# Attention: two units' weighted sums in one bank, one copy and one turn; the packs a place sooner, the causal masks in front of the wait for them

## The reference

```python
def _L0_attn_ref(x, W_Q, W_K, W_V, W_O):
    H, d_attn = 16, 8
    Q, K, V = x @ W_Q.T, x @ W_K.T, x @ W_V.T      # each then cut into 16 heads of 8
    attn = jnp.einsum('bhqd,bhkd->bhqk', Q, K) * scale
    attn = jnp.where(causal, attn, -jnp.inf)
    probs = jax.nn.softmax(attn, axis=-1)
    y = jnp.einsum('bhqk,bhkd->bhqd', probs, V)
    y = y.transpose(0, 2, 1, 3).reshape(Bx, Sx, Dm)
    return y @ W_O.T
```

## Time and profile before

| | |
|---|---|
| three runs | 1208.91, 1215.56, 1223.81 us; median 1215.56 |
| the profiled execution | 1208.36 us, of which its span is 1205.8 us |
| PE busy | 1106.7 us, 92% of the span |
| DVE busy | 1001.9 us, 83% |
| ACT busy | 789.6 us, 65% |
| POOL busy | 562.8 us, 47% |
| first mixture, attention, second mixture | about 330, 563 and 313 us (from 0, 330 and 893 us) |

### The profile page before, as it was taken

How to read it: one execution, slowest core, us unless ns; L and a number is a source line. 1 busy time by engine, 2 the same in 40 slices (tenths; PEclk the granted TensorE clock), 3 DMA queues, 4 the chain that set the end, 5 groups by cost and what they waited for, 6 DMA issues and landing times. The chain is left out here.

```text
span 1205.8 us, 31981 instructions
## 1 busy us (share of the span) xinstructions
PE 1106.7 (92%) x11588; PEld 683.5 (57%) x11588; DVE 1001.9 (83%) x2589; ACT 789.6 (65%) x1545; POOL 562.8 (47%) x722
## 2 busy tenths in 40 slices
PE   2899999999979989989999989989979999999998
PEld 1566666666525555555555555555545666666665
DVE  5889899898767888888888888888858898898985
ACT  4676767767526676676766766676646767666664
POOL 2566666666503233333333323333325666666655
PEclk9899999999968999999999999999988999999999
DMA  4442443432200000000000000000004434435333
GB/s 127 152 158 86 155 135 105 141 110 104 71 1 1 2 2 2 1 2 2 2 2 2 2 2 2 1 2 2 2 2 142 154 109 136 132 110 158 117 123 97
DMA packets 59865, 80.11 MB, mean 66 GB/s; under 512 B 5568, under 2 KB 26944, under 8 KB 59712
## 3 DMA queue, kind: packets, MB, share of 16 engines
q1 hardware_dynamic: 59712, 78.08, 20.5%
HBM read 73.34 MB, written 4.72 MB: 65 GB/s over the span
## 5 line engine op out<-in xcount | busy, mean ns | idle before, releaser
L696 POOL TENSOR_TENSOR h_lo<-h,h_hi 128x512 f16<-128x512 f32 x288 | 333.2, 1157 | 234.6 <-ACT h_hi L643 232.5
L1256 POOL TENSOR_SCALAR_AFFINE_SELECT probs_at<-probs_at 128x512 f32<-128x512 f32 x256 | 156.3, 634 | 343.9 <-ACT probs_at L1214 343.9
L1136 DVE TENSOR_REDUCE neg_max_at<-score_at 128x2 f16<-128x512 f32 (+1 forms) x384 | 253.9, 690 | 69.9 <-PE score_at L966 64.6
L1214 ACT ACTIVATE probs_at<-prob_at 128x512 f32<-128x512 f32 x384 | 201.7, 599 | 78.3 <-PE prob_at L998 76.4
L635 ACT ACTIVATE a<-a 128x512 f32<-128x512 f32 x256 | 149.0, 582 | 130.5 <-PE a L547 125.6
L435 DVE TENSOR_TENSOR prod<-a,gate_wide 128x512 f32<-128x512 f32 x256 | 175.9, 687 | 48.2 <-ACT a L635 46.6
L563 PE MATMUL y_b<-w_hi,h_hi 128*128 128x128 f16 x1152 | 208.2, 219 | 2.6 <-POOL h_lo L696 2.6
L563 PE MATMUL y_b<-w_lo,h_hi 128*128 128x128 f16 x1152 | 208.1, 219 | 0.0
L563 PE MATMUL y_b<-w_hi,h_lo 128*128 128x128 f16 x1152 | 208.0, 219 | 0.0
L643 ACT ACTIVATE h_hi<-h 128x512 f16<-128x512 f32 x288 | 179.5, 623 | 17.4 <-DVE h L445 16.7
L445 DVE TENSOR_TENSOR h<-prod,b 128x512 f32<-128x512 f32 x256 | 174.4, 681 | 5.3 <-issue 0.4
(11 more groups left out here) (139 smaller groups left out, 1960.0 us busy)
## 6 DMA issues: line engine op xcount, KB each, us to landing
gate_wide<-gate_rows SPq DMA_DIRECT2D x256, 256.0 KB, 5.4
x<-in_L_attn_x_dram SPq DMA_DIRECT2D x16, 256.0 KB, 6.1
out_dram<-x SPq DMA_DIRECT2D x16, 256.0 KB, 6.9
raw_w<-in_L_ffn_w_dram SPq DMA_DIRECT2D x3, 512.0 KB, 4.9
gate_rows<-gate_rows SPq DMA_DIRECT2D x32, 16.0 KB, 1.4
raw_w<-in_L_ffn_sw_dram SPq DMA_DIRECT2D x3, 64.0 KB, 3.6
raw_attn<-in_L_attn_W_Q_dram SPq DMA_DIRECT2D x1, 64.0 KB, 4.7
raw_attn<-in_L_attn_W_K_dram SPq DMA_DIRECT2D x1, 64.0 KB, 3.5
```

The source lines that it names most:

```text
L696: nc.gpsimd.tensor_tensor(h_lo[k][:, :], h[k][:, :], h_hi[k][:, :], ALU.subtract).then_inc(hlo_done, 1)
L1136: nc.vector.tensor_reduce(dst, src, AX.X, ALU.max, negate=True).then_inc(max_done, 1)
L1214: nc.scalar.activation(probs[j % 2][:, i, :], prob_bank[i][:, :], ACT.Exp, scale=SCALE).then_inc(exp_done, 1)
L1256: nc.gpsimd.affine_select(out=p, in_=p, compare_op=ALU.is_ge, fill=0.0, base=0, pattern=[[0, GROUPS], [1, P]], channel_multiplier=-1).then ...
```

## The change

Units j = 0, 1 and units j = 2, 3 of a sequence now share one filling of `o_bank`. `v_ones` keeps its size, but a head of an even unit has its 8 values and its one in the first 16 of its 32 columns and zeros in the other 16, a head of an odd unit the other way round (`v_places`). The odd unit's `weigh` adds to what the even one left; ACT copies after the odd unit only, `o_t` has half the size, and an `o` job has two transposes instead of four. The transposed heads then stand in another order: the division writes `y` in the order of the pairs, and W_O is loaded with its columns in that order, in two transfers with runs of 16 floats. In `PLACES` `o11` goes to the end of unit 2, and `Q00`, `K00`, `Q01`, `K01` move up by a place or more. The wait for the packs moves behind the masks (`packs_ready`).

```diff
+OUT_ROWS = ROWS // 2
...
-            sp.dma_start(self.raw["attn"][:, i, :], self.attn[n]).then_inc(self.loaded["attn"], DMA)
+            src, dst = self.attn[n], self.raw["attn"][:, i, :]
+            if n != "wo":
+                sp.dma_start(dst, src).then_inc(self.loaded["attn"], DMA)
+                continue
+
+            src = src.rearrange("p (g j d) -> p j g d", g=GROUPS, j=UNITS // 2)
+            dst = dst.rearrange("p (j g d) -> p j g d", g=GROUPS, j=UNITS // 2)
+            for j in range(UNITS // 2):
+                sp.dma_start(dst[:, j, :, :], src[:, j, :, :]).then_inc(self.loaded["attn"], DMA)
...
-PLACES = (((), ("q",), ("k",)), (("o10",), ("o11",), ("Q00",)), (("K00",), ("Q01",), ("K01",)),
+PLACES = (((), ("q",), ("k",)), (("o10",), ("Q00",), ("K00",)), (("Q01", "K01"), (), ("o11",)),
           (("m10", "m11"), ("y1",), ()),
           (("z1",), ("Q10",), ("K10",)), (("o00",), ("o01",), ("Q11",)), (("K11",), ("y0",), ("v",)),
           (("m00", "m01"), ("x",), ("z0",)))
...
+        def v_places(slot):
+
+            return v_ones[slot][:, :, :, :].rearrange("p t (n i) (k r) -> p (t n) (i k) r", i=2, r=OUT_ROWS)
...
-                    pe.wait_ge(o_done, c * 2 * UNITS + (b + 1) * UNITS)
+                    pe.wait_ge(o_done, (2 * c + b + 1) * UNITS // 2)
                     dst, done = begin(c, name)
-                    for j in range(UNITS):
+                    for i in range(UNITS // 2):
...
             def begin_scores(c, b, j, i):
 
-                if j == 0 and i == 0:
-
-                    wait_taken(pe, c, f"Q{b}1")
-                    wait_taken(pe, c, f"K{b}1")
...
+            def packs_ready(c, b, j):
+                if j == 0:
+                    wait_taken(pe, c, f"Q{b}1")
+                    wait_taken(pe, c, f"K{b}1")
...
                 parts = [begin_scores(later, later_b, later_j, i) for i in range(2)]
+                packs_ready(later, later_b, later_j)
...
                 pe.wait_ge(masked, unit * 2 + 2)
-                wait_count(pe, o_done, unit)
+                if j % 2 == 0:
+                    wait_count(pe, o_done, unit // 2)
...
-                                                start=(t == 0), stop=(t == 1), skip_group_check=True)
+                                                start=(t == 0 and j % 2 == 0), stop=(t == 1 and j % 2 == 1),
+                                                skip_group_check=True)
...
+                    o = src[:, 0:HEADS * OUT_ROWS].rearrange("p (h r) -> p h r", r=OUT_ROWS)
+                    nc.vector.reciprocal(inv[:, t, :], o[:, :, HEAD]).then_inc(inv_done, 1)
...
-                nc.vector.memset(v[:, :, HEAD + 1:ROWS], 0.0)
-                last = nc.vector.memset(v[:, :, HEAD:HEAD + 1], 1.0)
+                v = v_places(s)
+                nc.vector.memset(v[:, :, 1:3, :].rearrange("p n i r -> p n (i r)"), 0.0)
+                nc.vector.memset(v[:, :, 0:4:3, HEAD + 1:OUT_ROWS], 0.0)
+                last = nc.vector.memset(v[:, :, 0:4:3, HEAD:HEAD + 1], 1.0)
...
                 unit = c * 2 * UNITS + b * UNITS + j
+                if j % 2 == 0:
+                    return
                 act.wait_ge(pv_done, unit + 1)
```

More of the change, by code:

```diff
@@ L159, in load @@
         for i, n in enumerate(self.attn):
-            sp.dma_start(self.raw["attn"][:, i, :], self.attn[n]).then_inc(self.loaded["attn"], DMA)
+            src, dst = self.attn[n], self.raw["attn"][:, i, :]
[6 more added lines that the diff above has]
+                sp.dma_start(dst[:, j, :, :], src[:, j, :, :]).then_inc(self.loaded["attn"], DMA)
     def loads(self, name):
-        return {"router": 1, "attn": len(self.attn)}.get(name, 2) * DMA
+        return {"router": 1, "attn": len(self.attn) - 1 + UNITS // 2}.get(name, 2) * DMA
     def pool_consts(self, pool):
@@ L806, in attention_phase @@
         probs = [sb(f"probs{s}", [P, 3, CHUNK], F32) for s in range(2)]
-        o_t = [sb(f"o_t{s}", [P, UNITS, SEQ], F32) for s in range(2)]
-        inv = sb("inv", [P, 2, UNITS, GROUPS], F32)
+        o_t = [sb(f"o_t{s}", [P, UNITS // 2, SEQ], F32) for s in range(2)]
+        inv = sb("inv", [P, 2, HEADS], F32)
         y = sb("y", [P, 2, P], F32)
@@ L909, in job @@
                     b, t = int(name[1]), int(name[2])
-                    pe.wait_ge(o_done, c * 2 * UNITS + (b + 1) * UNITS)
+                    pe.wait_ge(o_done, (2 * c + b + 1) * UNITS // 2)
                     dst, done = begin(c, name)
-                    for j in range(UNITS):
-                        last = nc.tensor.transpose(dst[:, j * P:(j + 1) * P], o_t[b][:, j, t * P:(t + 1) * P],
+                    for i in range(UNITS // 2):
+                        last = nc.tensor.transpose(dst[:, i * P:(i + 1) * P], o_t[b][:, i, t * P:(t + 1) * P],
                                                    ident[:, :])
@@ L975, in scores @@
                     part = begin_scores(c, b, j, i)
+                    if i == 0:
+                        packs_ready(c, b, j)
                     for h in range(len(part[1])):
@@ L1111, in job @@
                     b, t = int(name[1]), int(name[2])
-                    o = src[:, :].rearrange("p (j g r) -> p j g r", j=UNITS, r=ROWS)
-                    nc.vector.reciprocal(inv[:, t, :, :], o[:, :, :, HEAD]).then_inc(inv_done, 1)
+                    o = src[:, 0:HEADS * OUT_ROWS].rearrange("p (h r) -> p h r", r=OUT_ROWS)
+                    nc.vector.reciprocal(inv[:, t, :], o[:, :, HEAD]).then_inc(inv_done, 1)
                     dve.wait_ge(inv_done, c * 4 + 2 * b + t + 1)
[L1115 to L1118, removed]
+                    last = nc.vector.tensor_tensor(y[:, t, :].rearrange("p (h d) -> p h d", d=HEAD), o[:, :, 0:HEAD],
+                                                   inv[:, t, :].unsqueeze(2).to_broadcast([P, HEADS, HEAD]), ALU.mult)
                 elif kind == "y":
@@ L1157, in _ @@
                 nc.vector.memset(neg_max[s][:, :, :, :, :].rearrange("p a b c d -> p (a b c d)"), 0.0)
-                v = v_ones[s][:, :, :, :].rearrange("p t h r -> p (t h) r")
-                nc.vector.memset(v[:, :, HEAD + 1:ROWS], 0.0)
-                last = nc.vector.memset(v[:, :, HEAD:HEAD + 1], 1.0)
+                v = v_places(s)
+                nc.vector.memset(v[:, :, 1:3, :].rearrange("p n i r -> p n (i r)"), 0.0)
+                nc.vector.memset(v[:, :, 0:4:3, HEAD + 1:OUT_ROWS], 0.0)
+                last = nc.vector.memset(v[:, :, 0:4:3, HEAD:HEAD + 1], 1.0)
             last.then_inc(buffers_set, 1)
@@ L1199, in job @@
                 elif kind == "v":
-                    nc.scalar.activation(v_ones[slot][:, :, :, 0:HEAD],
-                                         src[:, :].rearrange("p (t h d) -> p t h d", t=TILES, d=HEAD),
+                    nc.scalar.activation(v_places(slot)[:, :, 0:4:3, 0:HEAD],
+                                         src[:, :].rearrange("p (n i d) -> p n i d", i=2, d=HEAD),
                                          ACT.Copy).then_inc(done, 1)
@@ L1218, in take_o @@
                 unit = c * 2 * UNITS + b * UNITS + j
+                if j % 2 == 0:
+                    return
                 act.wait_ge(pv_done, unit + 1)
-                nc.scalar.activation(o_t[b][:, j, :], o_bank[:, 0:SEQ], ACT.Copy).then_inc(o_done, 1)
+                nc.scalar.activation(o_t[b][:, j // 2, :], o_bank[:, 0:SEQ], ACT.Copy).then_inc(o_done, 1)
             def turn(c, slot):
```

## The result

The changed kernel takes **1242.43 us** (median of 6 runs, 1229.1 to 1244.0); the kernel before, run beside it, 1213.91 us. The ratio, taken over the runs and not from the two medians, is 1.0191, with a 95% interval of 1.0155 to 1.0227: slower, though not certainly by 2%, where 1196 us and a range of 1181 to 1210 were forecast. The profiled execution took 1242.43 us, 34.1 us more than the one before.

The account below looks back on a forecast made before the run. PE (91% busy) looked like the bound, with DVE (83%) close behind. From 1208.4 us, -16.5 - 0.5 + 0.8 + 0.4 gave 1192.6; half of a 7.2 us median offset on top made 1196 us, range 1181 to 1210.

Parts of the forecast that it names:

- Units 1 and 2, the fewer transposes: Fewer transposes in `o10` and `o11` gain nothing, because PE then waits for DVE's maximum.
- the sum: Whole kernel: -16.5 - 0.5 + 0.8 + 0.4 = -15.8 us, so 1192.6 us for an execution like the profiled one.
- W_O's short runs: Rival: W_O's load delays x of the second chunk by some 27 us; 1219 us, up to 1226; chance 4%.
- The packs: Unit 2 to unit 3: packs ready sooner, 0.8 us a turn; 0.2 us of the wait turn into one for DVE.
- Unit 5: Two transposes fewer in `o00`, where PE sets the pace: 0.29 us a turn; nothing from `o01`.
- The last turn: No packs made there; fewer transposes and copies in front of unit 6's exponents: 0.5 us, between 0 and 1.
- W_O, +0.8 us: W_O's load in 64-byte runs delays the second chunk's x: 0.8 us added, between 0 and 1.8.
- the estimate of +0.3: W_O's load by the skill's packet overhead: 2.1 times its time before, some +0.3 us, the sum 0.5 us lower.
- The zeros of `v_ones`: Two instructions instead of one per buffer, in front of ACT's first job: 0.4 us added, between 0 and 0.8.
- What would show it: Signs: masks' `q_pack_at` wait from 14.2 to under 2 us, `neg_max_at` from 16.2 to 25; 128 transposes, 64 copies.
- The forecast's own range: Whole kernel, 1187 to 1203 us: 0.7 to 1.25 us a chunk, added parts at either end, offset 0 to 7.2.

Follow-up runs that it names:

- run 10: Changed kernel plus nine matmuls that nobody reads, in TensorE's wait in front of `o10`: 1194.38 us, ratio 0.9865 to the kernel before.
- run 2: Kernel before with only the new order (`PLACES`) and the masks in front of the pack wait: 1201.65 us, ratio 0.9889.
- run 3: Changed kernel in which each `o` job turns its two tiles twice, 128 useless transposes more: 1199.03 us, ratio 0.9870.
- run 5: Changed kernel with the second pair of transposes put back as waste in `o10` and `o11` alone: 1198.33 us, ratio 0.9867.
- run 1: Changed kernel with the old order and the masks behind the pack wait, so only the shared sums are left: 1242.45 us, ratio 1.0248.
- run 4: Kernel before with only two of four transposes in `o10` and `o11`, DVE reading the two tiles twice: 1250.86 us, ratio 1.0304.
- run 9: Kernel before plus six filling matmuls in front of `o10`, as a control: 1218.96 us, ratio 1.0035.
- run 11: Changed kernel plus six filling matmuls in front of `o10` and 24 of 512 columns before the attention's first `Q00`: 1197.93 us, ratio 0.9892.

## Why the prediction was wrong, by its steps

**The step that failed** is "Units 1 and 2, the fewer transposes": "I cost these edits at nothing; what is late next is the maximum." By waits this was right. From the turn's `xt_hi` copy to unit 2's heads it was 9.97 us before (604.90 less 594.93) and is 9.98 in run 10 (599.11 less 589.13). But the step took the granted clock of 1.00 in the earlier trace rows for a given, and the work that it removed was what held it. With the clock held, 15 turns take 487.8 us (run 10, 359.7 to 847.5); the changed kernel took 537.4. These 49.6 us are the term that the sum lacked. No rival named the clock, and the one that ended slower, W_O's short runs, had the wrong mechanism.

**The rest of the sum holds at full clock.** Run 10's 15 turns are 16.2 us shorter than before's 504.0, where 16.5 was forecast, and its profiled execution of 1192.2 us stands beside the sum of 1192.6. Its nine matmuls are its only difference from the changed kernel, and they are hidden. That the totals agree to 0.4 us is partly luck: the small terms below are not borne out one by one.

- *The packs, 0.8 us a turn.* From unit 2's heads to unit 3's it was 4.53 us (609.43 - 604.90) and is 3.70 in run 10: 0.83. The second mask now waits 0.21 us for DVE, as said. Run 2, with this part alone, gives 0.82.
- *Unit 5, 0.29 us.* A turn without a fall is 32.50 us with four transposes there (run 3) and 32.28 with two (runs 5 and 10): 0.22. Half of four transposes' time was too much to take off: `o10`'s two still take 0.34 us from start to start (616.90 - 616.56).
- *The last turn, 0.5 us.* From the last `xt_hi` copy to the end of the span it is 343.6 us before and 343.2 after, but 342.5 to 345.5 over all runs, with falls of the clock in it in both kernels: no run sizes so small a term.
- *W_O, +0.8 us.* W_O's loads on SP's queue before and in the changed kernel, and there DVE's first work on the second chunk:

```profile
8.38 0.43 SPq L160 DMA_DIRECT2D raw_attn<-in_L_attn_W_O_dram  x1
...
8.42 1.31 SPq L169 DMA_DIRECT2D raw_attn<-in_L_attn_W_O_dram  x2
...
13.15 0.87 DVE L77 BATCH_NORM_STATS2 stats<-x 128x6 f32<-128x128 f32 x4
```

  SP needs 0.88 us more for the two issues. DVE begins 0.20 us later than in the earlier trace rows, but at 13.67 and 13.79 in runs 1 and 3, with the new load, and at 13.58 in run 2, with the old one: the spread hides the term. So no run bears out or refutes the +0.8, nor the estimate of +0.3 from the Trainium skill ("DMA: Bandwidth & Descriptors", section "Why small descriptors are slow (HBM only)"). The attention's first memset starts at 331.04 us, and at 331.57 and 331.03 in runs 2 and 4, which load W_O as before, so nothing of it can be seen there.
- *The zeros of `v_ones`, +0.4 us.* From DVE's first memset to its first `q_stack`: 5.04 us before (330.31 to 335.35), 5.06 after, so the term is 0.02 us and not 0.4:

```profile
331.04 0.48 DVE L1176 MEMSET neg_max_at<- 128x512 uint32 x1 [0.47 <-PEq L237]
...
336.10 1.39 DVE L1118 TENSOR_TENSOR q_stack_at<-job_at,q_stack_at 64x512 f16<-64x512 f32 x2 [0.72 <-ACT q_stack_at L1209]
```

- *What would show it.* 128 transposes of `o_t` and 64 copies are left, and no row of PE's masks waiting for `q_pack_at` is among the large ones. Their waits for `neg_max_at` I put at 25 us or more; they are:

```profile
PE score_at L965 <- DVE neg_max_at L1155: 17.5, 28, 0.9
```

  That is hardly more than in the earlier trace rows, and at full clock it is no different (17.7 us in run 10): this size was off.
- *The range.* The forecast's own range does not add up: its parts give about 1189 us (1208.4 - 15 x 1.25 - 1) to about 1208 (1208.4 - 15 x 0.7 + 2.6 + 7.2), not 1187 to 1203. Both lie within 1181 to 1210, so the outcome is the same.

## What to carry to other kernels

Work that is taken from TensorE where it already waits is not free: where short waits stand close together, look at the granted clock, and put the loss of it into the sum as a rival with a price (2.5 to 4.6 us a fall in the changed kernel). Where an edit makes such a gap wider, fill the wait with matmuls that nobody reads, into a bank that no other engine reads at that time, and compare turns with and without a fall instead of medians alone.

## What was not expected of the hardware

- The granted clock fell to the lower level behind two waits of 0.53 and 0.86 us (changed kernel, run 4), and in run 9 behind one of 1.01 us, which the profiled execution of the kernel before had in every turn without a fall behind it.
- The fall shown, some 7 us long by its windows, makes `weigh` 1.76 times as long (1.51 against 0.86 us), but cost the turn only 2.5 us (34.75 against 32.28).
- At the start of the phase the clock was at 0.53 from 347 to 371 us though PE was busy for 21.92 of the 24 us (run 11).
